# Local attention: mask and row minimum in one VectorE instruction per head instead of a mask product on TensorE

## What is computed

```
def local_attention(q, k, v):                  # b, 8 heads, n = 2048, d = 64
    bq = q.reshape(b, h, w, WINDOW, d) * QK_SCALE
    bk, bv = (look_around(bk), look_around(bv))          # own window and the one before
    sim = jnp.einsum('bhwid,bhwjd->bhwij', bq, bk)
    mask = (i < j) | (i > j + WINDOW) | (j == -1)
    sim = jnp.where(mask, -jnp.finfo(sim.dtype).max, sim)
    attn = jax.nn.softmax(sim, axis=-1)
    out = jnp.einsum('bhwij,bhwjd->bhwid', attn, bv)
```

## Time and profile before

| | |
|---|---|
| median of 3 runs | 1342.97 us (1341.92 to 1343.94) |
| profiled execution, own time | 1346.67 us |
| its span, first to last instruction | 1344.20 us |
| mean granted TensorE clock | 0.945 |
| busy TensorE matmul | 1194.4 us (89%) |
| busy TensorE weight loads | 872.5 us (65%) |
| busy ScalarE | 896.4 us (67%) |
| busy VectorE | 895.0 us (67%) |
| busy GpSimd | 708.0 us (53%) |

### The profile page before, as it was taken

One profiled execution on the slowest core, in us unless ns is written; L12 is line 12 of the kernel. 1 busy time (PEld: TensorE's weight loads), 2 busy tenths in 40 slices (PEclk: granted clock), 3 DMA queues, 4 the chain that ended last, 5 costly groups with the idle time before them and its releaser, 6 DMA issues. The chain is left out here.

```text
span 1344.2 us, 34846 instructions
## 1 busy us (share of the span) xinstructions
PE 1194.4 (89%) x11174; PEld 872.5 (65%) x11183; DVE 895.0 (67%) x2443; ACT 896.4 (67%) x3049; POOL 708.0 (53%) x1170
## 2 busy tenths in 40 slices
PE   5899984999999988978999999979967999599997
PEld 3666761566666667964666666669946999444443
DVE  4689994677777756765777777647772001479998
ACT  3578873788888867856888888857763000277776
POOL 1579975788888852316888888823264000211112
PEclk9599996999999998998999999979978999799999
DMA  6000000122111112002121111100006886100000
GB/s 209 1 2 10 10 2 14 43 50 49 41 41 33 33 25 99 0 7 47 44 60 42 41 37 33 29 1 1 0 8 213 295 284 220 32 9 14 12 14 16
DMA packets 50824, 71.29 MB, mean 53 GB/s; under 512 B 25566, under 2 KB 36762, under 8 KB 46298
## 3 DMA queue, kind: packets, MB, share of 16 engines
q1 hardware_dynamic: 50682, 69.44, 18.0%
HBM read 46.20 MB, written 2.38 MB: 36 GB/s over the span
## 5 line engine op out<-in xcount | busy, mean ns | idle before, releaser
L1145 PE MATMUL psum<-wa_wqkv,wa_hT 128*128 128x512 f32 x384 | 201.6, 611 | 0.2 <-DVE wa_tmp L1020 0.2
L1106 ACT ACTIVATE wa_p<-psum,wa_nb 128x128 f32<-128x128 f32 x512 | 180.6, 372 | 2.3 <-DVE wa_nb L1032 2.3
L1000 POOL TENSOR_TENSOR wa_p<-wa_p,wa_rrs 128x512 f32<-128x512 f32 x128 | 133.3, 1041 | 51.4 <-DVE wa_rrs L1039 51.4
L1936 PE MATMUL psum<-ex_wT,ex_hT 128*128 128x512 f32 x256 | 132.5, 599 | 0.9 <-DVE ex_yw L1875 0.3
L1961 ACT ACTIVATE ex_yw<-psum,ex_w 128x128 f32<-128x128 f32 x384 | 103.0, 398 | 40.6 <-DVE ex_total L1892 33.7
L1032 DVE TENSOR_REDUCE wa_nb<-psum 128x4 f32<-128x512 f32 x128 | 82.5, 686 | 70.4 <-PE psum L1177 70.4
L1618 PE MATMUL psum<-cv_v,cv_toep 128*128 128x128 f32 x1024 | 117.5, 277 | 6.5 <-DMA cv_toep<-cv_zpad 6.5
L1618 PEld LDWEIGHTS psum<-cv_v,cv_toep 128*128 128x128 f32 x1024 | 116.7, 194 | 6.7 <-issue 6.7
L1106 ACT ACTIVATION_READ_ACCUMULATOR wa_p<-psum,wa_nb 128x1 f32 x512 | 109.0, 213 | 0.0
L1391 PE MATMUL psum<-ml_hnT,ml_w 128*128 128x128 f32 (+1 forms) x768 | 102.5, 285 | 0.0
L1116 ACT ACTIVATE wa_pT<-psum 128x512 f32<-128x512 f32 x128 | 77.7, 607 | 34.4 <-PE psum L1154 34.4
(11 more groups left out here) (263 smaller groups left out, 3393.9 us busy)
## 6 DMA issues: line engine op xcount, KB each, us to landing
cv_toep<-cv_zpad SPq DMA_DIRECT2D x32, 1024.0 KB, 5.5
wa_vm<-wa_v SPq DMA_DIRECT2D x127, 128.0 KB, 2.3
wa_tabs<-in_rotations_dram SPq DMA_DIRECT2D x2, 2048.0 KB, 8.2
x_rows<-in_L_attn_x_dram SPq DMA_DIRECT2D x4, 512.0 KB, 6.2
out_dram<-x_rows SPq DMA_DIRECT2D x32, 64.0 KB, 1.5
wa_rows<-y_rows SPq DMA_DIRECT2D x14, 128.0 KB
wa_rows<-y_rows SPq DMA_DIRECT2D x14, 127.0 KB
wa_wqkv<-in_L_ffn_wqkv_dram SPq DMA_DIRECT2D x2, 768.0 KB, 11.4
```

The lines of the kernel that those rows point to most:

```text
L1000: nc.gpsimd.tensor_tensor(p, p, cols_bc(rrs[:, t % 2, r, :], P), ALU.mult)\
L1106: e = nc.scalar.activation(pr[:, t % 2, r, h, :], sim_bank[r][:, P * h:P * h + P], ACT.Exp, bias=nb[:, t % 2, r, h:h + 1], accum_out=rs[:, ...
L1145: nc.tensor.matmul(bank, hT[:, t % 3, :], wqkv[:, INNER * k:INNER * k + INNER], start=True, stop=True).then_inc(done.sem, 1)
L1936: nc.tensor.matmul(bk[k], hT[:, u, :], wT[:, BANK * k:BANK * k + BANK], start=False, stop=True).then_inc(p_up(f"bank{k}"), 1)
```

## The change

The mask is kept in fp32 and no longer enters by TensorE. `scores` starts and ends each score product by itself. `row_max` does, for each of the four heads of a bank, one instruction that computes out = -(score + mask), writes it over the score in PSUM, and gives the minimum of the row as its accumulator. That minimum is the negated row maximum that the exponentials add; they now read the negated score with scale -1. The semaphore of the step is raised by the last of the four. The bf16 copies of identity and mask, and their casts, are gone.

```
-        self.bias32 = sb("wa_bias32", [P, 2, P])
-        self.bias = sb("wa_bias", [P, 2, P], BF16)
-        self.identb = sb("wa_identb", [P, P], BF16)
+        self.bias = sb("wa_bias", [P, 2, P])
...
     def vector(self, dve):
-        nc = self.c.nc
-        nc.vector.tensor_copy(self.identb[:, :], self.c.ident[:, :]).then_inc(self.pre, 1)
         self.wait_layer(dve, 0)
-        nc.vector.tensor_copy(self.bias[...], self.bias32[...]).then_inc(self.pre, 1)
         self.scale_tables(dve)
...
+    MAX_FLOAT = float(np.finfo(np.float32).max)
...
                 def row_max(r):
                     def f(t):
                         p_sim.wait(dve, t)
-                        nc.vector.tensor_reduce(nb[:, t % 2, r, :], sim_bank[r].rearrange("p (h k) -> p h k", k=P),
-                                                AX_X, ALU.max, negate=True).then_inc(v_nb[r].sem, 1)
+                        edges = bias[:, (t % NT + NT - 1) // NT, :]
+                        for h in range(PAIRS):
+                            s = sim_bank[r][:, P * h:P * h + P]
+                            m = nc.vector.tensor_tensor_reduce(out=s, in0=s, in1=edges, scale=-1.0, scalar=MAX_FLOAT,
+                                                               op0=ALU.add, op1=ALU.min,
+                                                               accum_out=nb[:, t % 2, r, h:h + 1])
+                        m.then_inc(v_nb[r].sem, 1)
...
-                dve.wait_ge(given.pre, 4 * l + 6)
+                dve.wait_ge(given.pre, 4 * l + 4)
...
                             e = nc.scalar.activation(pr[:, t % 2, r, h, :], sim_bank[r][:, P * h:P * h + P], ACT.Exp,
-                                                     bias=nb[:, t % 2, r, h:h + 1],
+                                                     bias=nb[:, t % 2, r, h:h + 1], scale=-1.0,
                                                      accum_out=rs[:, t % 2, r, h:h + 1])
...
                     for r in range(2):
                         a_exp[r].wait(pe, t - 1)
-                        nc.tensor.matmul(sim_bank[r].rearrange("p (h k) -> p h k", k=P), identb[:, :],
-                                         rows_bc(bias[:, (t % NT + NT - 1) // NT, :], PAIRS), start=True, stop=False,
-                                         skip_group_check=True)
                     for h in range(PAIRS):
                         for r in range(2):
...
-                                             own_and_before(t, s, h), start=False, stop=h == PAIRS - 1,
-                                             skip_group_check=True)
-                            m = nc.tensor.matmul(out[hi, :], qT[s, t % 2, h, hi], kT[s, t % 2, h, :], start=False,
-                                                 stop=h == PAIRS - 1, skip_group_check=True)
+                                             own_and_before(t, s, h), start=True, stop=True)
+                            m = nc.tensor.matmul(out[hi, :], qT[s, t % 2, h, hi], kT[s, t % 2, h, :], start=True,
+                                                 stop=True)
```

More of the change, by code:

```diff
@@ L830, in first_loads @@
     def first_loads(self, sp, y_done):
-        sp.dma_start(self.bias32[...], self.c.inp["window_bias"]).then_inc(self.loaded, 16)
+        sp.dma_start(self.bias[...], self.c.inp["window_bias"]).then_inc(self.loaded, 16)
         self.load_layer(sp, 0)
@@ L879, in windowed_attention @@
     wqkv, wo, tabs = given.wqkv, given.wo, given.tabs
-    bias, identb, rows, vm = given.bias, given.identb, given.rows, given.vm
+    bias, rows, vm = given.bias, given.rows, given.vm
+    MAX_FLOAT = float(np.finfo(np.float32).max)
     V_RING, VM_RING = 5, given.VM_RING
```

## The result

| | median us | runs | against before |
|---|---|---|---|
| before | 1342.25 | 5 (1341.92 to 1343.94) | |
| changed kernel | 1337.16 | 5 (1336.35 to 1341.26) | 0.9965 [0.9948, 0.9981] |

The account below looks back on a forecast made before the run. TensorE bounds the kernel now; the mask product's saving becomes a wait in a two-tile loop through VectorE and GpSimd. Turn 8.31 us against 8.29, +1.1 us in all: 1342.97 + 1.1 = 1344.1 us, range 1330 to 1362.

Parts of the forecast that it names:

- The bound and the slack: Local attention: TensorE bounds; GpSimd's scale_p1 would allow turn_p1 at 337.15, TensorE comes at 337.48, slack 0.33 us.
- The loop: Minima, rotate_q, residual, reciprocal, GpSimd's scale_p0 to scale_p1, turn_p1, one TensorE pass; spans two tiles, turn 8.31 us.
- X: Start-to-start time of one of the eight 128-element VectorE minima: 0.275 us, from bounds of 0.19 and 0.39.
- the forecast's own formula: Two turns last 14.42 us + 8X, so one turn is 7.21 + 4X.
- the floor: Loop from turn_p1 through second exponentials, reciprocal and scale_p1: a turn cannot be shorter than 7.97 us, whatever X is.
- the chance of 0.42: Forecast case: X between 0.26 and 0.30, turn 8.25 to 8.41, -2 to +7 us, 1341 to 1350.
- rival B: VectorE's accumulator nearly free, X 0.19 to 0.26, or GpSimd's loop shorter: down to -18 us, 1325; chance 0.27.
- The mask product: Removing TensorE's two bf16 mask products per tile saves 0.48 us of its turn, between 0.42 and 0.52.
- rival D: Removed product gains TensorE nothing; score products wait for second exponentials or weight loads: turn 8.55, +15 us; chance 0.05.
- Rival C: VectorE's accumulator read waits for its instruction to finish, X 0.30 to 0.39: up to +27 us, 1370; chance 0.26.
- The estimate from the Trainium skill: VectorE minima priced by the page's fixed cost for small tiles: X 0.32 us, turn 8.49, 11 us slower.
- The signs in the profile: Turn near 8.3 us, TensorE about 94% busy, 2.2 us from first minimum to rotate_q, GpSimd waiting over 0.62 us.

Follow-up runs that it names:

- the 512-element pair: Changed kernel with one 512-element minimum per bank instead of four of 128, one common minimum for all four heads: 1324.71 us, 0.9866 of before.
- the other run with the clip on VectorE: Changed kernel with eight minima, VectorE's residual moved behind rotate_k, and the clip moved from GpSimd to the end of VectorE's order: 1324.86 us, 0.9864 of before.

## Why the prediction was right or wrong

- **The bound and the slack** (TensorE, with GpSimd's scale_p1 close behind turn_p1): right. After the change turn_p1 is released by it in 62 of 64 tiles.
- **The loop**: right in its links and in its length. The chain from the end of the minima to turn_p1 took 6.40 us, forecast 6.47, and TensorE's pass 7.99, forecast 7.95; the two errors nearly cancel. With the measured 1.96 us for 8X, the forecast's own formula gives (14.42 + 1.96) / 2 = 8.19; measured 8.18. With 1.21 it goes under the floor (7.94 measured, 7.97 forecast), with the product kept it gives 8.43 (8.40), with 0.53 more 8.45 (8.44). That turns would alternate was not foreseen; a loop over two tiles sets only the mean of two.
- **The step that failed: the price of one minimum, X**, 0.275 us forecast, 0.245 measured. The formula multiplies it by 4, so 0.03 of error is 0.12 us per turn, 6.7 us in all: with the measured X the forecast would have been 1342.97 + (8.19 - 8.29) x 56 = 1337.4, against 1337.16; that these agree to 0.2 us is partly luck, since the runs lie between 1336.35 and 1341.26. The accumulator's read was priced by ScalarE's 0.08 and by VectorE's MATCH_VALUE_LOAD; on VectorE it costs an estimated 0.05 to 0.06, by the 0.19 of the earlier trace rows (0.05 too in the 512-element pair: 0.65 against 0.60). Both are comparisons with another operation; no run has this instruction without its accumulator. What was then added on top, "a little for a longer wind-up", rested on no row. With X as sensitive as that, the chance of 0.42 on a band of 0.04 us around one value was too high: the measurement lies in the band of rival B, 0.19 to 0.26.
- **The mask product**: forecast 0.48, from bounds of 0.42 and 0.52; measured 0.44 (from project_q to the first score product 1.39 us before, 337.85 to 338.80 = 0.95 after). The first score products don't wait for the second exponentials; rival D is out.
- **Rival C** (the read waits until its instruction has finished, 0.39): out, the read starts 0.22 after an instruction that lasts 0.30. **The estimate from the Trainium skill** (VectorE: DVE Perf Modes, The TRN2 errata; 0.32 by its fixed cost): the measurement is 0.245, so taken as a price from start to start that fixed cost is too high here; that small tiles pay per instruction agrees (0.70 us between eight and two). That an instruction with an accumulator counts as two (the same page of the Trainium skill, Two Vector instructions with no wait between them) agrees as well: 512 reads stand behind 512 instructions.
- **The signs in the profile**: GpSimd's wait grew from 0.62 to 0.95; TensorE is busy 95.9%, forecast 94%; 1.96 us from the first minimum to rotate_q, forecast 2.2; the clock stayed at 1.00 in the stage.
- **Outside the change**: the stages before, between and behind local attention differ from run to run by a few us (219 to 226 us up to the first rotate_q in these profiles). The spans' 5.1 us and the stages' 4.9 agree here partly by chance, since 3.0 us came from the unchanged first stage and 2.8 were lost again between and behind the stages.

## What to carry to other kernels

In a pipeline whose engines work in a fixed order, the cost of an instruction is decided by the loop that it stands in, divided by the number of tiles that the loop spans: 0.53 us cost 0.26 in one place and nothing in another. Taking work from the engine that is the bound gains only down to the next loop (0.35 of 0.44 here), and what is added elsewhere must be weighed against that loop's slack; if it stands in the loop, look first whether it can be moved behind the instruction that the others wait for. Where a forecast multiplies one unmeasured duration by four, give its rivals as much chance as the bounds of that duration, and add nothing to it that no row supports.

## What the runs showed of the hardware

A VectorE instruction of 128 elements with mask add, scale and row minimum, PSUM to PSUM, starts every 0.245 us (an estimated 0.05 to 0.06 of it for the accumulator); one of 512 elements every 0.61 to 0.65.

The clip of 128 x 16 elements takes 0.25 us on GpSimd, but 0.64 on VectorE (last fence above). It starts at 332.98 and ends at 333.62, and GpSimd's scale_p1 ends at 332.55 + 1.04 = 333.59. In the other run with the clip on VectorE the two ends are 330.18 + 0.64 = 330.82 and 329.75 + 1.04 = 330.79:

```profile
329.75 1.04 POOL L991 TENSOR_TENSOR wa_p<-wa_p,wa_rrs 128x512 f32<-128x512 f32 x1
...
330.18 0.64 DVE L1023 TENSOR_SCALAR wa_ss<-wa_ss 128x16 f32<-128x16 f32 x1
```

In the filling turns of both runs the same clip lasts 0.22 to 0.81 us, by when it starts, and it too ends 0.02 to 0.04 us after an instruction of GpSimd. So VectorE seems to be held until GpSimd's instruction is done. The Trainium skill (SBUF — State Buffer, Who interferes with whom) says that of a VectorE instruction in a two-port mode that is issued while GpSimd holds the shared ports; both rows agree with it. That the clip runs in such a mode is not shown, and no run here tried it by itself. In the steady turns it cost nothing, since it stands in VectorE's wait for the scores: the turn is 7.93 with the clip and without.
